# A delta-rule layer on one core: the last join of each 64-row half replaced by a solve in two halves, copies and waits moved, and work added to TensorE's last group

## The reference

```python
h = _rms(x, norm_in_w); h = silu(causal_conv(h))          # 4 taps
q, k, v = heads(h @ Wq), heads(h @ Wk), heads(h @ Wv)     # q, k to unit length
drive = heads(h @ Wspike)
def step(carry, ins):
    s, mem = carry
    qt, kt, vt, dt, at, bt = ins
    mem = DECAY * mem + dt
    spike = (mem > THR)
    mem = mem - spike * THR
    alpha = sigmoid(at + asp * spike)
    beta = sigmoid(bt[..., None] + sum(spike * bsp))
    active = (sum(abs(spike)) > 0)
    alpha = where(active > 0, alpha, 1); beta = beta * active
    s = s * alpha[..., None]
    pred = einsum('bhk,bhkv->bhv', kt, s)
    s = s + (beta * kt)[..., None] * (vt - pred)[:, :, None, :]
    return (s, mem), einsum('bhk,bhkv->bhv', qt, s)
y = head_norm(y) @ Wo * gate; y = x + y
y = y + silu(z @ Wff1) * (z @ Wff3) @ Wff2                # z = rms(y)
```

## Time and profile before

| | us |
|---|---|
| median of 3 runs | 1461.54 (1457.33 to 1476.28) |
| the profiled execution | 1458.59 |
| its span, first to last instruction | 1456.9 |
| mean granted clock of TensorE, share of 2.4 GHz | 0.868 |
| PE busy, whole span | 1115.5 (77%) |
| DVE busy | 1032.8 (71%) |
| ACT busy | 625.4 (43%) |
| POOL busy | 57.4 (4%) |

### The profile page before, as it was taken

The page is one execution under the profiler, slowest core; times in us unless marked ns, Lnnn a source line. Parts: engine busy times, 40 slices in busy tenths (PEclk is TensorE's granted clock), DMA queues, the critical chain, the costliest instruction groups (busy, mean ns, idle before and its releaser), DMA issues. The chain is left out here.

```text
span 1456.9 us, 23383 instructions
## 1 busy us (share of the span) xinstructions
PE 1115.5 (77%) x7956; PEld 821.2 (56%) x7956; DVE 1032.8 (71%) x3377; ACT 625.4 (43%) x860; POOL 57.4 (4%) x74
## 2 busy tenths in 40 slices
PE   2087777228888988889888898887876888889885
PEld 1043232117777877778777787777732635446381
DVE  4779999978788787887878878788241736454451
ACT  2247677323333433334333343333333656474522
POOL 2000000010000000000000000000100102011100
PEclk9579887558999999999999999999878998998956
DMA  2002233310100100101010010110110000000000
GB/s 84 0 1 87 105 127 145 116 51 16 36 25 33 36 14 36 35 22 36 14 36 36 22 36 14 36 36 7 30 39 0 1 0 8 0 8 1 8 1 7
DMA packets 27211, 49.09 MB, mean 34 GB/s; under 512 B 4246, under 2 KB 8919, under 8 KB 27162
## 3 DMA queue, kind: packets, MB, share of 16 engines
q1 hardware_dynamic: 25642, 47.02, 9.3%
q10 hardware_dynamic: 1520, 1.48, 0.4%
HBM read 26.47 MB, written 22.02 MB: 33 GB/s over the span
## 5 line engine op out<-in xcount | busy, mean ns | idle before, releaser
L920 PE MATMUL ps<-delta_tm,drive 128*128 128x128 f32 x768 | 106.7, 295 | 3.9 <-DVE delta_zb L1046 3.8
L920 PEld LDWEIGHTS ps<-delta_tm,drive 128*128 128x128 f32 x768 | 98.2, 205 | 9.4 <-DVE delta_zb L1046 5.9
L931 PE MATMUL ps<-delta_tt,delta_xf 128*128 128x64 f32 x768 | 101.4, 275 | 0.0
L929 PE MATMUL ps<-delta_xf,delta_tt 128*128 128x64 f32 x768 | 99.8, 273 | 0.0
L929 PEld LDWEIGHTS ps<-delta_xf,delta_tt 128*128 128x128 f32 x768 | 94.7, 194 | 0.0
L779 ACT ACTIVATE delta_xf<-ps 128x256 f32<-128x256 f32 (+1 forms) x128 | 49.1, 383 | 106.0 <-PE ps L920 86.0
L1203 DVE TENSOR_TENSOR delta_tm<-delta_tm,ps 128x256 f32<-128x256 f32 x96 | 40.3, 419 | 76.6 <-PE ps L931 75.6
L931 PEld LDWEIGHTS ps<-delta_tt,delta_xf 128*128 128x128 f32 x768 | 93.5, 192 | 0.0
L892 PEld LDWEIGHTS ps<-delta_kq_up,delta_arena 64*128 64x128 f32 x1024 | 74.1, 225 | 22.3 <-DVE delta_diag L1161 15.1
L892 PE MATMUL ps<-delta_kq_up,delta_arena 64*128 64x128 f32 x1024 | 80.3, 317 | 1.4
L551 DVE SCALAR_TENSOR_TENSOR kept<-mem 128x32 f32<-128x32 f32 x384 | 73.2, 191 | 1.6 <-PEq L79 1.0
(11 more groups left out here) (368 smaller groups left out, 2628.9 us busy)
## 6 DMA issues: line engine op xcount, KB each, us to landing
kq_store<-prep_unit SPq DMA_DIRECT2D x8, 1024.0 KB, 4.2
zb_store<-prep_zb_cols SPq DMA_DIRECT2D x8, 1024.0 KB, 5.7
delta_zb<-zb_store SPq DMA_DIRECT2D x16, 512.0 KB, 3.4
delta_kq<-kq_store SPq DMA_DIRECT2D x16, 512.0 KB, 3.2
v_store<-prep_v_rows SPq DMA_DIRECT2D x4, 1024.0 KB, 6.6
delta_v<-v_store SPq DMA_DIRECT2D x16, 256.0 KB, 2.6
out<-post_rows SPq DMA_DIRECT2D x4, 256.0 KB, 2.3
setup_wmod<-in_L_wmod ACTq DMA_DIRECT2D x2, 384.0 KB, 3.9
```

The source lines that it names most:

```text
L920: ins = eng.matmul(m.ps[:, 4 + n, P * (h % 4):P * (h % 4) + P], bt[s][:, h, :], m.tm[:, h, :], start=True, stop=True)
L929: eng.matmul(m.ps[:, 6 + n, HD * (h % 4):HD * (h % 4) + HD], m.tt[:, h, :], cols(m.xf[:, h, :], 0), start=True, stop=True)
L931: ins = eng.matmul(m.ps[:, 6 + n, 256 + HD * (h % 4):256 + HD * (h % 4) + HD], m.xf[:, h, :], cols(m.tt[:, h, :], 1), start=True, stop=True)
```

## The change

In the delta phase:

- The join of 64 is gone. The joins of 8, 16 and 32 stay, and the third makes only its second product (line 942 of the new kernel), since nothing reads `tm` any more. The system is solved in two halves of 64 rows: PE solves rows 0 to 63 (`solve_half(i, 0)`), ACT copies them (`solved_half`), PE multiplies them by the corner block `bt[64]` (`carried`), DVE subtracts that from rows 64 to 127 of `rest`, and PE solves those (`solve_half(i, 1)`). The output is made in two halves as well (`out_half`).
- The products of the state with the keys (`seen_by_k`) stand between the two parts of the third join, and banks 0, 1 and 3 take what went to banks 2, 3, 4, 5 and 0.
- The query blocks of 32 and 64 are copied by ACT (`far_queries`, six instructions) and no longer by DVE (four copies and two short fills). The write of `tt` is in two parts, one for each group of heads.
- DVE makes the spikes of chunk i+2 after the first join of chunk i, where it made those of chunk i+1 before the first row. The log gates and their scan stand before DVE's part of the first join; the exponential of the gates on ACT stands before its copies of `X8`, and the logarithm between them.
- DVE's loop has 14 chunks, and the last two are written out.

In the post phase:

- `contract` waits for each slice on its own.
- In passes that have both parts, the copy of the first weights by ACT stands ahead of the gate's logarithm, and on PE `weights_to_columns(i, 0)` and `values(i, 0)` stand ahead of parts of the gate's sums.
- In the last pass PE makes 16 more products of 128x512 into bank 7, which nothing reads (`unread`).

Without a few names, waits and the last chunk's calls, and with twelve columns of indent taken off, the diff is:

```diff
 LEVELS = [1, 2, 4] + UPPER
-JOINS = [8, 16, 32, 64]
...
+def front_gates_ln(n):
     eng.wait_ge(scalar_front, fact.at("zb_e", n))
     eng.activation(zbf, zbf, ACT.Ln, bias=1.0).then_inc(scalar_front, fact.one("zb_ln"))
...
+def far_queries(i):
+    eng.wait_ge(vector_back, vec.at("up16b", i))
+    for n, x in enumerate(HALVES):
+        hs = slice(n, H, 2)
+        ps = m.ps[:, BANK_OF[64] + n, :].rearrange("p (h a c) -> p h a c", h=4, a=2)
+        eng.activation(m.a_qk[0:HD, hs, HD:P], ps[0:HD, :, 1, :], ACT.Copy).then_inc(scalar_back, act.one(f"qk64{x}"))
+    for n, x in enumerate(HALVES):
+        hs = slice(n, H, 2)
+        ps = m.ps[:, BANK_OF[32] + n, :].rearrange("p (h a c) -> p h a c", h=4, a=2)
+        eng.activation(m.a_qk[0:32, hs, 32:64], ps[0:32, :, 1, 0:32], ACT.Copy)
+        eng.activation(m.a_qk[64:96, hs, 96:128], ps[64:96, :, 1, 32:64], ACT.Copy).then_inc(scalar_back, act.one(f"qk32{x}"))
...
+def solved_half(i, which):
+    ks = slice(HD * which, HD * which + HD)
...
-        eng.activation(m.tt[0:HD, hs, HD:P], src, ACT.Copy, scale=-1.0).then_inc(scalar_back, act.one(f"XT64{x}"))
+        eng.wait_ge(tensor_back, pe.at(f"u{which}{x}", i))
+        eng.activation(m.u_rows[ks, 256 * n:256 * n + 256], m.ps[ks, 4 * which + n, 0:256], ACT.Copy).then_inc(scalar_back, act.one(f"u{which}{x}"))
...
 with eng.Fori(0, NT - 1) as i:
     spread_rows(i)
     far_blocks(i)
+    far_queries(i)
     transposed(i)
+    front_gates(i + 1)
     join(i, 8)
-    front_gates(i + 1)
+    front_beta(i + 1)
     join(i, 16)
-    front_beta(i + 1)
     front_lift2(i + 1)
     join(i, 32)
     front_lift(i + 1)
-    last_join(i)
+    solved_half(i, 0)
     end_rows(i)
-    solved_rows(i)
     front_lift3(i + 1)
+    solved_half(i, 1)
     output(i)
     front_late(i + 1)
 spread_rows(NT - 1)
...
+    eng.wait_ge(scalar_back, act.before("qk64b", n))
     eng.matmul(m.ps[:, 2, :], m.bd[:, :], m.spk[:, :, :].rearrange("p c t -> p (c t)"), start=True, stop=True).then_inc(tensor_front, fpe.one("count"))
...
     for n, x in enumerate(HALVES):
-        eng.wait_ge(vector_back, vec.at(f"up32{x}", i))
-        eng.wait_ge(scalar_back, act.at(f"bt32{x}", i))
+        eng.wait_ge(scalar_back, act.at(f"qk32{x}", i))
+        eng.wait_ge(vector_back, vec.at(f"tt{x}", i))
...
+def seen_by_k(i):
+    eng.wait_ge(vector_back, vec.at("kq_all", i))
     for h in range(H):
         ks, cs = head(h)
-        ins = eng.matmul(m.ps[:, 2 + h % 2, HD * (h // 2):HD * (h // 2) + HD], m.kq_all[ks, 0, cs], m.state[ks, h // 2, :], start=True, stop=True)
+        ins = eng.matmul(m.ps[:, h % 2, HD * (h // 2):HD * (h // 2) + HD], m.kq_all[ks, 0, cs], m.state[ks, h // 2, :], start=True, stop=True)
     ins.then_inc(tensor_back, pe.one("seen"))
...
+def solve_half(i, which):
+    ks = slice(HD * which, HD * which + HD)
     eng.wait_ge(vector_back, vec.at("rest", i))
-    eng.wait_ge(scalar_back, act.at("XT64b", i))
-    for h in range(H):
-        ins = eng.matmul(m.ps[:, 5, HD * h:HD * h + HD], m.tt[:, h, :], m.rest[:, HD * h:HD * h + HD], start=True, stop=True)
-    ins.then_inc(tensor_back, pe.one("solved"))
+    for n, x in enumerate(HALVES):
+        eng.wait_ge(vector_back, vec.at(f"sub{x}" if which else f"XT{x}32", i))
+        for h in range(4 * n, 4 * n + 4):
+            ins = eng.matmul(m.ps[ks, 4 * which + n, HD * (h % 4):HD * (h % 4) + HD], m.tt[:, h, ks], m.rest[:, HD * h:HD * h + HD], start=True, stop=True)
+        ins.then_inc(tensor_back, pe.one(f"u{which}{x}"))
+def carried(i):
+    eng.wait_ge(tensor_back, pe.at("read", i))
+    for n, x in enumerate(HALVES):
+        eng.wait_ge(scalar_back, act.at(f"u0{x}", i))
+        for h in range(4 * n, 4 * n + 4):
+            ins = eng.matmul(m.ps[:, n, HD * (h % 4):HD * (h % 4) + HD], bt[64][0:HD, h, :], m.u_rows[0:HD, HD * h:HD * h + HD], start=True, stop=True)
+        ins.then_inc(tensor_back, pe.one(f"w{x}"))
...
+def out_half(i, which):
+    us, ts = slice(0, HD + HD * which), slice(HD * which, HD * which + HD)
     for h in range(H):
-        ks, cs = head(h)
-        ins = eng.matmul(m.ps[ks, 6 + h % 2, cs], m.u_rows[:, HD * h:HD * h + HD], m.a_qk[:, h, :], start=False, stop=(h >= H - 2))
-    ins.then_inc(tensor_back, pe.one("out"))
+        ks = slice(HD * (h % 2), HD * (h % 2) + HD)
+        c = P * (h // 2) + HD * which
+        ins = eng.matmul(m.ps[ks, 6 + h % 2, c:c + HD], m.u_rows[us, HD * h:HD * h + HD], m.a_qk[us, h, ts],
+                         start=False, stop=(which == 1 and h >= H - 2))
+    if which:
+        ins.then_inc(tensor_back, pe.one("out"))
...
+def state(i):
+    end_keys(i)
+    solve_half(i, 0)
+    seen_by_q(i)
+    carried(i)
+    out_half(i, 0)
+    eng.wait_ge(scalar_back, act.at("kend", i))
+    solve_half(i, 1)
+    eng.wait_ge(scalar_back, act.at("u1b", i))
+    out_half(i, 1)
+    update(i)
...
-def blocks(i, ahead=True):
+def blocks(i):
     upper(i, 8, "a")
     upper(i, 8, "b")
-    if ahead:
-        front_spikes(i + 1)
-    r = 0
-    for s in UPPER[1:]:
-        for x in HALVES:
-            r += 1
-            row(i, r)
-            row_sum(i, r)
-            upper(i, s, x)
-    row(i, 7)
-    row_sum(i, 7)
+    for r in range(1, BASE):
+        row(i, r)
+        row_sum(i, r)
+        if r < 3:
...
+def carried(i):
+    eng.wait_ge(vector_back, vec.at("rest", i))
+    for n, x in enumerate(HALVES):
+        eng.wait_ge(tensor_back, pe.at(f"w{x}", i))
+        r = m.rest[HD:P, 256 * n:256 * n + 256]
+        eng.tensor_tensor(r, r, m.ps[HD:P, n, 0:256], ALU.subtract).then_inc(vector_back, vec.one(f"sub{x}"))
...
-with eng.Fori(0, NT - 1) as i:
+def chunk(i, ahead):
     base(i)
     blocks(i)
     front_z(i + 1)
     front_sums(i + 1)
     front_late(i)
+    front_decay(i + 1)
     join(i, 8, "a")
+    front_mid(i + 1)
     join(i, 8, "b")
-    front_decay(i + 1)
+    front_splits(i + 1, UPPER[:1])
+    if ahead:
+        front_spikes(i + 2)
     join(i, 16, "a")
-    front_mid(i + 1)
-    front_splits(i + 1, UPPER[:1])
+    front_splits(i + 1, UPPER[1:3])
     join(i, 16, "b")
-    front_splits(i + 1, UPPER[1:])
+    front_splits(i + 1, UPPER[3:])
     front_toend(i + 1)
+    rest(i)
     join(i, 32, "a")
     front_beta(i + 1)
     join(i, 32, "b")
     front_base(i + 1)
-    front_upper(i + 1, UPPER[:1])
-    rest(i)
-    front_upper(i + 1, UPPER[1:3])
+    carried(i)
+    front_upper(i + 1, UPPER[:2])
     keep(i)
-    front_upper(i + 1, UPPER[3:])
+    front_upper(i + 1, UPPER[2:])
     update(i)
...
+def gate_silu_ln(i):
     eng.wait_ge(mix_scalar, mact.at("g_e", i))
     eng.activation(m.gu_e[:, :], m.gu_e[:, :], ACT.Ln, bias=1.0).then_inc(mix_scalar, mact.one("g_ln"))
...
     if mix:
         gate_silu(j)
+    if win:
+        weights_out(i, 0)
+    if mix:
+        gate_silu_ln(j)
         y_logs(j, 0)
     if win:
-        weights_out(i, 0)
...
+def unread(n):
+    for _ in range(n):
+        eng.matmul(m.ps[:, 7, :], m.ones[:, :], cols(m.hT, 0), start=True, stop=True)
+def contract(bank, w, src, done, value, made):
     for c in range(4):
+        eng.wait_ge(*made(c))
         ins_ = eng.matmul(m.ps[:, bank, :], w[:, c, :], src[:, c, :], start=(c == 0), stop=(c == 3))
     ins_.then_inc(done, value)
...
-    contract(6, m.wff2, m.hid_a, mix_tensor, mpe.one("ff2"))
+    eng.wait_ge(mix_scalar, mact.at("a2_e", i))
+    contract(6, m.wff2, m.hid_a, mix_tensor, mpe.one("ff2"), lambda c: (mix_vector, mvec.at(f"a{c}", i)))
...
-    contract(7, m.w2, m.hid_a, mix_tensor, mpe.one("w2"))
+    eng.wait_ge(mix_scalar, mact.at("gelu2", i))
+    contract(7, m.w2, m.hid_a, mix_tensor, mpe.one("w2"), lambda c: (mix_scalar, mact.at(f"gelu{c}", i)))
...
+        unread(1)
     if win:
         scores(i, 1)
     if mix:
-        y_sums(j, 0)
+        y_sums(j, [0])
+    else:
+        unread(2)
     if win:
         weights_to_columns(i, 0)
+    if mix:
+        y_sums(j, [1])
+    else:
+        unread(1)
+    if win:
         scores(i, 2)
-    if mix:
-        y_sums(j, 1)
+        values(i, 0)
+    if mix:
+        y_sums(j, [2, 3])
     if i == -1:
         gate(j)
         scales()
     if win:
-        values(i, 0)
         weights_to_columns(i, 1)
     if mix and win:
         gate(j)
+    if not mix:
+        unread(1)
     if win:
         scores(i, 3)
         own(i, 0)
...
             gated_hidden(j, f)
         gated_out(j)
+    if not mix:
+        unread(1)
     if win:
         windows_out(i)
     if mix:
         mix_mean("n1", j)
+    else:
+        unread(1)
     if win:
         win_mean("n3", i)
     if mix:
         mix_var("n1", j)
+    else:
+        unread(2)
     if win:
         win_var("n3", i)
+    if not mix:
+        unread(3)
     if mix:
         gelu_hidden(j, range(3))
     if win:
         win_mean("n4", i)
     if mix:
         gelu_hidden(j, range(3, NF))
+    else:
+        unread(2)
     if win:
         win_var("n4", i)
     if mix:
         gelu_out(j)
+    else:
+        unread(2)
     if win:
```

168 lines of the change are left out of this document (67 added, 101 removed).

## The result

The changed kernel takes 1406.43 us (median of 4 runs, 1402.89 to 1414.77), against 1461.99 us before (4 runs on the same chip, 1457.33 to 1476.28). The ratio is 0.961, with a 95% interval from 0.953 to 0.969. I had forecast 1374 with a range from 1346 to 1410: the sign is right and the time lies inside, but close to its upper end, and outside the range that I had given my own mechanism (1356 to 1394). The profiled execution took 1408.76 us for a span of 1407.0, so 49.8 less than that of before, where the sum had 85 (by the medians it is 55.6).

The account below looks back on a forecast made before the run. Neither engine fills the delta phase: DVE paces a chunk up to the first join, PE the joins and rest. 1458.6 less 59 (delta), 5.6, 4.5 and 16 (post) gives 1373.5, predicted 1374; range 1346 to 1410, own mechanism 1356 to 1394.

Parts of the forecast that it names:

- The rows stage: Early in the delta chunk: four gaps after row sums lose their query copy, 1.6 us per chunk; `tt` starts at 11.7.
- The join of 8 at 14.7, behind the gate sums: Delta chunk: PE's first join waits for DVE's gate sums and starts at t = 14.7, 2.0 earlier than before.
- The join of 32 at 26.1: Delta chunk: still 11.4 us from the join of 8, so the join of 32 starts at t = 26.1.
- `carried` at 1.88, not 1.04: Delta chunk, corner-block product: 16 weight loads cost 1.88 us, since all heads lie on rows 0 to 63; bound 1.04.
- The end of the chunk, 41.0 at the full level: Delta chunk: PE's chain ends at 39.2, DVE's at 40.9, so the next chunk starts at 41.0.
- So DVE is late, by 1.7: End of the delta chunk: DVE ends 1.7 us behind PE, with two of its pairs now behind the subtraction.
- I take 41.4: Delta chunk length, between 41.0 and 42.0 at the lower clock: 3.7 us gained per chunk, 59 us over 16.
- `gated_out`, 5.6 us: Post phase, four mixer passes: PE's wait of 1.41 for the last slice before this contraction goes, 5.6 us.
- The weights' copy ahead, 4.5 us: Post phase, three passes with both parts: 1.5 of PE's 2.14 wait for ACT's weights copy saved, 4.5 us; bounds 0 and 6.4.
- The last pass, 16 us: Last post pass: unread products lift PE from the lower clock to a granted clock near 1, saving 16 us.
- that of the hand-overs: Rival for the delta chunk: hand-overs between engines cost more, chunk 43.4, gain only 27 there, 1406 us; chance 0.17.
- Slower* rival: Rival: PE's new waits late in the chunk bring the lower clock into the next joins, +12 per chunk, 1565 us; chance 0.02.

Follow-up runs that it names:

- experiment 8: Changed kernel with the odd heads' products of `carried` taken from rows 64 to 127 (constants) into an unread bank: 1379.37 us, ratio 0.943.
- experiment 5: Changed kernel with one of DVE's four pairs of scaled keys and queries moved into its wait for `carried`: 1407.24 us, ratio 0.958.
- experiment 9: Changed kernel with the mixer's last two sums of squares ahead of the window's first products with the values again: 1399.66 us, ratio 0.954.
- both_early: Changed kernel with narrowed gate-sum wait, ACT's gate functions and DVE's scan later around the join of 8, and last mixer sums ahead of values: 1372.33 us, ratio 0.939.
- all_three: both_early with one pair of scaled keys and queries also moved ahead of DVE's subtraction: 1368.12 us, ratio 0.936 to the kernel before.
- wait_only: Changed kernel with PE's gate-sum wait only ahead of the second group's products in the join of 8, other queues unchanged: 1394.69 us, ratio 0.954.

## Why the prediction was right or wrong

The direction, the order of the terms and the places were right; the size of the gain was 50 of 85. That 1406 lies inside 1346 to 1410 is luck: my own mechanism had 1356 to 1394, and the range went to 1410 for a rival that did not come true. Two of the signs that I had named failed, the chunks 41 to 42 apart (42.85) and the granted clock near 1 in the last pass (0.86). By phases, in the profiled executions: the delta phase 35.6 instead of 59, the post phase 14.2 instead of 26.

- **The rows stage: right.** `row` follows `row_sum` after 0.22 (599.37 to 599.59); `tt` starts at t = 11.8 (11.7 forecast). Undone, it costs 1.52 per chunk (1.6). ACT's copies end at t = 11.2 and the transposes wait for `tt`, not for them; PE does wait 0.2 to 0.55 for one of them ahead of the count of the spikes, in time that it would have waited anyway (1.15 for `tt` follows).
- **The join of 8 at 14.7, behind the gate sums: right** (14.8, a wait of 0.99). What I did not ask is whether that wait had to be there: it is needed for one of two banks.
- **The join of 32 at 26.1, the state's part over at 29.2, the join at 31.0: right** (26.0, 29.2, and 31.0 by the next row of PE).
- **`carried` at 1.88, not 1.04: right** (1.92 to 1.99), and the reason given fits experiment 8, which changed the bank as well.
- **The end of the chunk, 41.0 at the full level: nearly right, and for an incomplete reason.** 41.55 was measured. The 0.5 is there by `carried` (34.5 instead of 34.0), and the rest follows. "So DVE is late, by 1.7" holds up to the update, by 1.4 (PE's ends at 39.8, DVE's starts at 41.2), but PE's chain goes on into the base products of the next chunk, which leaves 0.6 at the full level and none at the lower one (experiment 5).
- **The step that failed: "The next chunk starts at 41.0, or at 42.0 where the spread rows run at the lower clock. I take 41.4".** I set a chunk with 0.4 of lower level against one of 45.1, in which it cost 0.96; the gain of work alone was 44.12 - 41.55 = 2.6 per chunk, and I had credited 3.7. Measured at 42.85, the chunk is 1.45 over the forecast: 0.5 is work and waits, 0.9 is the level (1.30 and not 0.4). 16 x 1.45 = 23, which is the whole miss of the phase (59 - 35.6). The long chunks show where it falls: the spread rows and the whole join of 8, 3.68 instead of 2.05. The rest falls in a new place, the end of the chunk: from the join of 16 to the next spread rows it is 26.5 at the full level, but 27.0 to 27.2 in eight of 15 chunks, where the kernel before has 28.0 in all.

```profile
723.28 2.04 PE L893 MATMUL ps<-drive,delta_block_ones 128*128 128x512 f32 x2 [2.91 <-DVE drive L1158]
...
733.47 3.68 PE L928 MATMUL ps<-delta_tm,drive 128*128 128x128 f32 x16 [0.99 <-DVE delta_zb L1066]
```

- **`gated_out`, 5.6 us: right at its place** (the wait of 1.41 is gone in each pass), but taken back in the mixed passes.
- **The weights' copy ahead, 4.5 us: wrong.** The third scores do start 0.9 earlier (9.13 behind the first, and 10.06 before). But PE does the values ahead of the last sums of squares, so ACT's logarithms (1185.79) and then its second copy of the weights (1189.97) come later, and the fourth scores wait 1.83 instead of 0.34: the wait has moved. I had bounded this term by 0 from below; with `gated_out` in it the first two passes gained 0.3 and lost 0.1, and experiment 9 gives 1.7 back in the second and 0.4 in the first.
- **The last pass, 16 us: the mechanism right, the size 13.4**, with 12.7 of it shown to be the unread products. Some 17 us of the pass still read 0.5 (1365 to 1382). Other kernels with the same last pass had 66.8, so the size is 11 to 13.

The rival nearest in time was that of the hand-overs (1406, at 0.17). Its mechanism is not what happened: in the full-level chunk all hand-overs together cost 0.5 more than I had put in, where it had 2.0. The *Slower* rival came nearer, with new waits that bring the lower level, and had too high a price (12 per chunk; measured 0.34 more than before). The rows put that at the end of the chunk; that the new waits are its cause is not shown.

What stays open: what makes the level fall in a given chunk. Its cost differs by 9 us between traces of the same delta code, filling the longest wait freed the spread rows of it and not the join of 8, and the third pass takes 84.4 or 87.8 with the same instructions. For a kernel like this that is a part of the time that I could bound but not predict.

## What to carry to other kernels

Take a phase apart into its shortest repetition, which is work and waits, and the mean above it, which is the clock; forecast both, and subtract like from like. Where a chain of hand-overs ends a loop body, follow each engine into the next body until the instruction that is really waited for. And ask of every wait which part of its reader needs it, and which queues stand behind it: here a wait of 1 us per chunk was needed for one bank of two, but taking it away only moved it to ACT until ACT's and DVE's queues were put in another order as well.

## What the runs showed that I had not expected

- The same delta code took 42.28 to 42.85 per chunk in four traces, at shortest chunks that agree within 0.03. In both_early and all_three the lower level costs 0.5 and 0.7 per chunk.
- The lower level can cost nothing: 1.4 us more of busy PE (3.50 instead of 2.06 on line 892 of the kernel before) in front of a wait left the next step where it was, to 0.01.
- In `carried`, instructions on different halves of the rows start 0.01 apart, and 16 of them take 1.11; on the same half each starts 0.11 behind the last and they take 1.99. Products on all rows, alternating between the two halves of the result, gain as well (0.64 against 1.15 for 16 instructions).
- A removed wait of PE of 0.99 for DVE came back as one of 0.90 for ACT within 3 us (wait_only), with the next join starting at the same time to 0.01.
